# Attention output normalised in 32x32-block transposes on VectorE, in place of two full transposes on TensorE

## The reference

```
x = x + attn_a(layernorm(x))
x = x + ffn(layernorm(x))
x = x + attn_b(layernorm(x))          # causal, rotary
x = x + ffn(layernorm(x))

attn: scores = q k^T / sqrt(16); p = softmax(scores)
      out[b, n, (h d)] = sum_m p[b, h, n, m] v[b, m, h, d];  return out @ out_w^T (+ out_b)
ffn:  gate = sigmoid((x Wq^T) routers^T);  leaf = product of the gates on the path, 256 leaves
      return (leaf @ leaf_values) Wout_w^T + Wout_b
```

## Time and profile before

| | |
|---|---|
| runs | 1141.99, 1144.35, 1144.99 us; median 1144.35 |
| profiled execution | 1141.19 us, span from the first to the last instruction 1139.5 us |
| TensorE clock granted, mean | 0.99 of 2.4 GHz |
| busy: PE, DVE, ACT, POOL | 1075.6, 883.5, 761.6, 307.0 us |
| chain that ended last: PE, DVE, ACT | 59%, 22%, 7% of the span |

### The profile page before, as it was taken

The page is one execution under the profiler, slowest core; times in us unless marked ns, Lnnn a source line. Parts: engine busy times, 40 slices in busy tenths (PEclk is TensorE's granted clock), DMA queues, the critical chain, the costliest instruction groups (busy, mean ns, idle before and its releaser), DMA issues.

```text
span 1139.5 us, 18953 instructions
## 1 busy us (share of the span) xinstructions
PE 1075.6 (94%) x6164; PEld 543.1 (48%) x6164; DVE 883.5 (78%) x2481; ACT 761.6 (67%) x1565; POOL 307.0 (27%) x339
## 2 busy tenths in 40 slices
PE   5899999999999999999999999999999898989986
PEld 3323444444445444554455544454444555545544
DVE  4887787787868897687977878788886878777844
ACT  3577767677776678765777767776776666666562
POOL 3011110114213150222403151131513526262210
PEclk9999999999999999999999999999999999999999
DMA  8150501402205131321305023051311313022001
GB/s 240 49 128 19 130 20 50 99 20 85 83 20 130 38 107 43 99 70 38 111 20 149 20 66 102 19 131 35 103 50 40 110 38 122 28 85 65 20 20 37
DMA packets 79778, 80.97 MB, mean 71 GB/s; under 512 B 13088, under 2 KB 68672, under 8 KB 79680
## 3 DMA queue, kind: packets, MB, share of 16 engines
q1 hardware_dynamic: 79616, 79.73, 24.6%
q0 software_dynamic: 64, 0.03, 0.0%
HBM read 20.71 MB, written 8.39 MB: 26 GB/s over the span
## 4 chain that ended last, share of the span: by engine, by line
PE 59%; DVE 22%; ACT 7%; issue 4%; SPq 3%; POOL 2%; DMA 1%; POOLq 0%; DVEq 0%; ACTq 0%
PE ps_work L1304 13%; PE ps_out L1213 12%; PE ps_max L1167 11%; PE ps_key L1189 11%; DVE neg_max L916 8%; PE ps_work L1343 7%; ACT probs L797 4%; PE ps_work L1269 3%; DVE scratch L1073 3%; DVE ps_max L912 2%; SPq L538 2%; DVE scratch L1103 2%; DVE scratch L1076 2%; ACT turned_block L818 2%; DVE moments L1021 1%
## 5 line engine op out<-in xcount | busy, mean ns | idle before, releaser
L797 ACT ACTIVATE probs<-ps_key 128x512 f32<-128x512 f32 (+3 forms) x1024 | 515.4, 520 | 297.2 <-PE ps_key L1189 291.5
L916 DVE TENSOR_REDUCE neg_max<-ps_max 128x1 bf16<-128x512 f32 x512 | 336.9, 684 | 86.5 <-PE ps_max L1167 85.2
L1167 PE MATMUL ps_max<-k_stack,q_stack 96*128 96x512 bf16 (+3 forms) x1024 | 347.0, 345 | 24.0 <-DVE neg_max L912 10.0
L1189 PE MATMUL ps_key<-q_stack,k_stack 97*128 97x512 bf16 (+3 forms) x1024 | 348.4, 343 | 16.0 <-ACT probs L797 10.5
L912 DVE CUSTOM_DVE_ANT_0 ps_max<-ps_max,mask_b 128x128 f32<-128x128 f32 (+3 forms) x512 | 247.1, 504 | 105.5 <-PE ps_max L1167 102.7
L1213 PE MATMUL ps_out<-probs,v_ones 128*32 128x512 f32 (+3 forms) x2048 | 233.8, 529 | 0.6 <-POOL probs L688 0.6
L1167 PEld LDWEIGHTS ps_max<-k_stack,q_stack 96*128 96x128 bf16 x1024 | 99.4, 97 | 277.1 <-DVE neg_max L916 109.8
L688 POOL TENSOR_SCALAR_AFFINE_SELECT probs<-probs 128x512 f32<-128x512 f32 x128 | 82.2, 643 | 402.3 <-ACT probs L797 401.7
L1189 PEld LDWEIGHTS ps_key<-q_stack,k_stack 97*128 97x128 bf16 x1024 | 100.9, 99 | 139.7 <-ACT probs L797 87.6
L1213 PEld LDWEIGHTS ps_out<-probs,v_ones 128*32 128x32 f32 x2048 | 40.4, 108 | 73.7 <-issue 65.3
L912 DVE DVE_READ_ACCUMULATOR2_ANT neg_max<- 128x1 bf16 x512 | 72.8, 142 | 0.0
(11 more groups left out here) (93 smaller groups left out, 1254.1 us busy)
## 6 DMA issues: line engine op xcount, KB each, us to landing
k_stack<-k_part SPq DMA_DIRECT2D x108, 128.0 KB, 2.4
q_stack<-q_part SPq DMA_DIRECT2D x108, 128.0 KB, 2.4
k_stack<-k_part SPq DMA_DIRECT2D x42, 256.0 KB
q_stack<-q_part SPq DMA_DIRECT2D x42, 256.0 KB
x_in<-in_x SPq DMA_DIRECT2D x8, 512.0 KB, 3.9
q_stack<-shift_rows SPq DMA_DIRECT2D x256, 1.0 KB, 1.7
x_again<-in_x SPq DMA_DIRECT2D x8, 512.0 KB, 3.9
spill<-x_plain SPq DMA_DIRECT2D x8, 512.0 KB, 2.8
```

The source lines that it names most:

```text
L797: act.activation(probs[step % RING][:, j, q0:T], ps_key[slot % 2][:, 0:T - q0], ACT.Exp, scale=SCALE).then_inc(on["exp_done"], 1)
L916: dve.tensor_reduce(out=dst, in_=src, axis=AX_X, op=ALU.max, negate=True)\
L1167: pe.matmul(dst[:, 0:keys], q_stack[n % 2][0:SPLIT_ROWS, h, P * qt:P * qt + P], k_stack[n % 2][0:SPLIT_ROWS, h, 0:keys], start=True, stop= ...
L1189: pe.matmul(ps_key[slot % 2][:, 0:T - q0], k_stack[n % 2][0:STACK_ROWS, h, P * kb:P * kb + P], q_stack[n % 2][0:STACK_ROWS, h, q0:T], star ...
```

## The change

The output is no longer turned to full token rows and back by TensorE. VectorE transposes `out_raw` in 32x32 blocks (`turn_out`, slots 7, 23, 39, 55) to `out_rows`: each block holds 32 tokens down and one head's 16 features and denominator across. One slot later `divide` takes the reciprocals and multiplies into one half of `divided[half]`, where the features of two groups lie side by side. One slot after every second group (slots 9 and 41 in all phases but the first) `turn_back` transposes `divided[half]` in 32x32 blocks to `turned_out`, which the projection reads directly. Since the features now come out in another order, the rows of `a_o` and `b_o` are loaded in that order, by 8 DMAs each at slot 30 of phases 0 and 1; the one product that needs `a_o` in plain order, `bias_fold`, and the first projection read a copy `first_out` loaded at slot 2 of phase 0. The work banks have fewer users. Some steps move by a slot or more in the tables.

```diff
-TURN_LAG = MIX_LAG + 5
+OUT_TURN = 2
...
-    ("bias_input", 0, (), 1), ("bias_input", 1, (), 3), ("turn_attended", 0, (13,), 14),
-    ("turn_attended", 1, (14,), 15), ("project_out", 0, (18, 19), 20), ("moments", 0, (), 21),
-    ("project_out", 1, (21, 22), 23), ("moments", 1, (), 23), ("spread", 0, (), 24), ("turn_block", 0, (30,), 31),
+    ("bias_input", 0, (), 1), ("bias_input", 1, (), 3), ("project_out", 0, (18, 19), 20), ("moments", 0, (), 21),
+    ("project_out", 1, (21, 22), 23), ("moments", 1, (), 23), ("spread", 0, (), 28), ("turn_block", 0, (30,), 31),
...
+def half_of(n, g):
+
+    return (g % 2, g // 2) if n == 0 else (g // 2, g % 2)
...
+                if slot == 30 and n < len(PLACED):
+                    for k in range(KC):
+                        by_place = w[PLACED[n]][P * k:P * k + P, :].rearrange("(e j d) n -> j e d n", e=2, j=GROUP)
+                        for j in range(GROUP):
+                            sp.dma_start(weights[PLACED[n]][COLS * j:COLS * j + COLS, k, :], by_place[j])\
+                              .then_inc(placed_loaded[n], DMA)
...
-            def divide(n, g, bank):
...
-                dve.wait_ge(on["out_turned"], count.next("out_turned"))
-                dve.reciprocal(inverse[:, :, :], turned[:, :, :, DH]).then_inc(on["inverse_done"], 1)
...
+            def turn_out(n, g):
+
+                if count.some("divided"):
+                    dve.wait_ge(on["divided"], count.of("divided"))
+
+                dve.wait_ge(on["out_ready"], count.next("out_ready"))
+                dve.transpose(out_rows[:, :], out_raw[g % 2][:, :]).then_inc(on["out_turned"], 1)
+                count.add("out_turned")
+
+            def divide(n, g):
+                half, odd = half_of(n, g)
...
+                dve.wait_ge(on["out_turned"], count.of("out_turned"))
+                rows = by_block(out_rows)
+                dve.reciprocal(inverse[:, :], rows[:, :, DH]).then_inc(on["inverse_done"], 1)
...
+                dve.tensor_tensor(by_block(divided[half])[:, :, DH * odd:DH * odd + DH], rows[:, :, 0:DH],
+                                  inverse[:, :].unsqueeze(2).broadcast_to([P, T // COLS, DH]), ALU.mult)\
+                   .then_inc(on["divided"], 1)
...
+            def turn_back(n, g):
+                half, odd = half_of(n, g)
+                if odd:
+
+                    dve.wait_ge(on["divided"], count.of("divided"))
+                    dve.transpose(turned_out[:, half, :], divided[half][:, :]).then_inc(on["attended"], 1)
+                    count.add("attended")
...
-            def turn_out(g, begun, bank):
...
-                for qt in range(TILES):
-                    last = pe.transpose(bank[:, P * qt:P * qt + P], out_raw[g % 2][:, P * qt:P * qt + P], ident[:, :])
...
-            def turn_attended(m, i, n, bank, parts):
-
-                pe.wait_ge(on["attended"], count.of("attended"))
-                turn_tiles(attended, i, bank)
...
+                rows(turned_out, weight, i, bank, D, "x_ready", parts, "added_full", "attended")
```

More of the change, by code:

```diff
@@ L390, in by_tile, with by_block @@
             return bank[:, :].rearrange("p (t n) -> p t n", t=2)
[L392 to L393 removed]
+        def by_block(rows):
+            return rows[:, :].rearrange("p (b c) -> p b c", c=COLS)
         on = {name: sem(name) for name in EVENTS}
@@ L949, in core @@
                     largest(n, at)
-                if out_due(n, slot) is not None:
-                    divide(n if slot >= GROUP_SLOTS else n - 1, out_due(n, slot), bank_of["turn_out", n, slot])
+                for lag, step in ((OUT_TURN, turn_out), (OUT_TURN + 1, divide), (OUT_TURN + 2, turn_back)):
+                    due = out_due(n, slot, lag)
+                    if due is not None:
+                        step(*due)
             def opening():
@@ L981, in closing @@
             def closing():
-                divide(PHASES - 1, GROUPS - 1, bank_of["turn_out", PHASES, 0])
+                for step in (turn_out, divide, turn_back):
+                    step(PHASES - 1, GROUPS - 1)
             def add(m, i, bank, src):
@@ L1216, in mixed @@
                 last.then_inc(on["mixed_done"], 1)
-            def turn_out(g, begun, bank):
-                pe.wait_ge(on["out_ready"], count.of("out_ready", begun))
-                take(bank, "attended")
-                for qt in range(TILES):
-                    last = pe.transpose(bank[:, P * qt:P * qt + P], out_raw[g % 2][:, P * qt:P * qt + P], ident[:, :])
-                last.then_inc(on["out_turned"], 1)
             def core(n, slot):
@@ L1228, in core @@
                     ahead(n, at)
-                if out_due(n, slot) is not None:
-                    turn_out(out_due(n, slot), 1, bank_of["turn_out", n, slot])
                 by_key(n, slot)
@@ L1294, in turn_leaves, with rows @@
                 turn_tiles(leaf_probs[(LEVELS - 1) % 2], i, bank)
-            def rows(turned, weight, i, bank, width, read, parts, full):
+            def rows(turned, weight, i, bank, width, read, parts, full, made="turned"):
                 if 0 in parts:
-                    pe.wait_ge(on["turned"], count.of("turned"))
+                    pe.wait_ge(on[made], count.of(made))
                     take(bank, read)
@@ L1311, in project_out @@
             def project_out(m, i, n, bank, parts):
-                rows(turned_block, weights["b_o" if causal(m) else "a_o"], i, bank, D, "x_ready", parts, "added_full")
+                if i == 0 and 0 in parts:
+                    count.add("attended", KC)
+                if m > 0 and i == 0 and 0 in parts:
+                    pe.wait_ge(placed_loaded[1 if causal(m) else 0], DMA * KC * GROUP)
+                weight = first_out if m == 0 else weights["b_o" if causal(m) else "a_o"]
+                rows(turned_out, weight, i, bank, D, "x_ready", parts, "added_full", "attended")
                 added[i] = count.of("x_ready")
```

78 lines of the change are left out of this document (38 added, 40 removed).

## The result

The changed kernel took 1150.2 us (median of 7 runs, 1147.37 to 1152.17) against 1144.03 us for the kernel before (7 runs, 1141.09 to 1146.1). The ratio is 1.0049, 95% interval 1.0032 to 1.0065: 5.6 us slower, where 10 us faster had been forecast. Slower by over 0.3% had a chance of 0.22. The time lies inside the stated range of 1115 to 1155 us, but that range took in both signs, so this says nothing for the forecast.

What follows compares the result with a forecast made beforehand. No single engine was taken to set the pace: TensorE in some stretches, VectorE in others. Gains of 20.5 us less 11 us of added VectorE work gave about 10 us less, 1144.35 to 1134 us; range 1115 to 1155.

Steps and rivals of the forecast that it cites:

- The price of the block transpose: One 128x512 f32 block transpose on VectorE, absent from the trace, was taken at 0.65 us, between bounds 0.60 and 0.83.
- The gain where TensorE paces: TensorE's removed transpose sets on the chain, 0.44 us each: 13.3 - 0.67 + 1.8 us, of 42.2 us in all.
- Slots 7 to 9 of plain phases: VectorE's 1.33 us of new work fits barely into 1.9 us idle; 0.15 us booked in 20 places, 3 us.
- The 0.65 us booked for slots 23 and 39: Added VectorE transposes where VectorE is late (slot 23) or ahead of the next norm's statistics (slot 39): 12 places, 7.8 us.
- Moved table steps and the freed work banks I book at nothing either way: Steps moved in the slot tables and work banks with fewer users: no gain or cost booked.
- the 4.9 us of ScalarE's copies: ScalarE loses 32 copies; ten on the chain at 0.49 us, most after slot 9 of causal phases, gain 4.9 us.
- Slots 55 to 57 in all phases, 23 to 25 in causal ones: VectorE has 2.5 to 6.5 us to spare per group there, so its added transposes cost nothing.
- the end, 1.2 us less: Serial path at the very end: turning, dividing and turning back falls from 3.36 to 2.2 us.
- the clock, named as a sign and booked at nothing: Granted clock below 0.99 as TensorE works less would show the prediction wrong; no time booked.
- VectorE's term: Cost of VectorE's added block transposes on the path: 3 + 7.8 = 10.8, about 11 us.
- Rival 4: Slower, 1161 us: the block transpose is a half-rate pass of 1.22 us; chance 0.22 for the slower side as a whole.

Runs made afterwards that it cites:

- the short block transposes: The changed kernel with both kinds of VectorE block transpose cut to 32 of their 512 columns: ratio 0.988 to the kernel before, 1128.3 us.

## Why the prediction was wrong

**Right.** The price of the block transpose: 0.65 us, measured 0.70 in duration and 0.63 to the next start. The gain where TensorE paces: 0.44 us in three of the four plain groups from slot 53 (0.34 in the last), and 12.8 us over the kernel for 14.4 summed. Slots 7 to 9 of plain phases: the work did fit there, and the groups from slot 5 fell by 0.51 us. The 0.65 us booked for slots 23 and 39 was of the right size: 0.8 us in plain groups from slot 21, and 0.44 in causal ones from slot 37 once `leaves` 1 is back.

**Failed: "Moved table steps and the freed work banks I book at nothing either way".** This step made the kernel slower: `leaves` 1 one slot later costs 5.5 us, and without that the ratio is 1.0001. The forecast's 10 us faster had failed beside it, for the reasons below. Its four short operations had filled a wait of VectorE for TensorE; moved, they leave it idle there and lengthen a row of operations ahead of a maximum. I had read neither which idle time a moved step stood in nor what it is joined with.

**Failed: the 4.9 us of ScalarE's copies.** The count was short to begin with: the chain has 12 such pieces ahead of the closing part, not 10, two in each of phases 1, 2, 4, 6, 8 and 10. In phases 1 and 2 the groups from slot 5 did get 1.0 us shorter each, which is the size of two copies. In causal phases 4 to 10, where eight of them lay (8 x 0.49 = 3.9 us), the groups from slot 5 should have lost about 1 us each, and instead grew by 0.02. ScalarE in the changed kernel, causal phase 6, in order of time:

```profile
473.97 0.63 ACT L903 ACTIVATE q_part<-scratch 128x512 bf16<-128x512 f32 x1 [1.08 <-DVE scratch L1141]
...
476.76 0.63 ACT L903 ACTIVATE q_part<-scratch 128x512 bf16<-128x512 f32 x1 [0.43 <-DVE scratch L1141]
```

In the place of its copies ScalarE now waits for VectorE's remainder of the split (L1141). VectorE and, under it, GpSimd at that place:

```profile
471.52 0.71 DVE L979 STREAM_TRANSPOSE turned_out<-divided 128x512 f32<-128x512 f32 x1
...
472.60 1.34 DVE L1141 TENSOR_TENSOR scratch<-scratch,q_part 128x512 f32<-128x512 f32 x1
```

```profile
470.89 2.50 POOL L782 TENSOR_TENSOR k_part<-scratch,k_part 128x512 bf16<-128x512 f32 x2
473.35 1.08 POOL L706 TENSOR_SCALAR_AFFINE_SELECT probs<-probs 128x512 f32<-128x512 f32 x1
```

The remainder took 0.83 us here before, most of it in a gap of GpSimd's work, and 1.34 now. With the short block transposes it took 0.69 and started 0.74 us earlier, counted from the copy, ScalarE didn't wait for it, and the group came out 0.89 us shorter than before. ScalarE's exponential stands behind that wait and TensorE's next product behind the exponential, in the changed kernel and with the short transposes:

```profile
476.23 0.23 PE L1227 MATMUL ps_key<-q_stack,k_stack 97*128 97x128 bf16 x1 [0.92 <-ACT probs L815]
```

```profile
469.97 0.23 PE L1232 MATMUL ps_key<-q_stack,k_stack 97*128 97x128 bf16 x1 [0.34 <-ACT probs L820]
```

So VectorE's new work took this gain. How much of it by its own length and how much through the slower remainder no run separates.

**Failed: "Slots 55 to 57 in all phases, 23 to 25 in causal ones: TensorE paces ... Cost nothing."** It held for slots 55 to 57 (-0.34 to -0.44 us a group). At slot 23 it didn't: with the moved steps back, the causal groups from slot 21 are 0.23 us longer than before where they should be 0.44 shorter, and moving the transpose off slot 23 gave those 0.67 us back. The 2.5 us to spare that I read were a sum over 16 slots; at slots 20 to 24 there was less to spare than the transpose and the division take.

**Failed: the end, 1.2 us less.** It was 1.5 us more: the path is 0.9 us shorter and the projection, at half clock, 2.6 longer.

**Failed: the clock, named as a sign and booked at nothing.** The prediction said that it is wrong if the granted clock falls below 0.99. It was 0.981 in the profiled execution, for 0.990 before, and 0.978 in the median, which by the line of the kernel before is as much as the whole loss. Where one and the same group of phases 4 to 10 has a stretch at half clock in one trace and none in another with the same places, it is 0.9 to 1.25 us longer (from slot 37) or 1.4 to 1.7 (from slot 5).

**The sum again.** 15.6 us lie between forecast and result. Of these 5.5 are `leaves` 1, 3.9 ScalarE's copies, 2.7 the end and 1.6 the sets of transposes, together 13.7. The other 1.9 would then be VectorE's term, 12.9 for the 11 booked; that is a remainder and wasn't measured, and since phases 1 and 2 gave back up to 2.0 us of copies where 1.0 was booked, it may as well be 2.9. The clock is no further term beside these: 2.6 of the 2.7 us at the end are clock and about 1 of the 5.5, and part of the remainder may be. Rival 4 had the right side by the wrong mechanism, and none of the rivals was a moved step.

**What stays open.** Where the clock falls differs between executions of one kernel, and each kernel has one trace; so how much of each ratio is clock is known only as the line over 90 executions has it, and what of the lower clock is cause and what effect isn't known. The moved steps were tried apart; the new order in which the work banks are taken, booked at nothing in the same sentence, was not.

## What to carry to other kernels

Where a diff changes operations and also moves steps of a schedule, price each move by itself: which idle time the step had filled, and what stands behind it in its new place. Here one step of four short operations cost 5.5 us, where the fastest version gained 11.9. Room on an engine is read in the slots in which new work lands, not as a sum over the stage; with the four steps of causal phases back in their old places, one group's transposes four slots later and TensorE kept busy ahead of the last projection, the same algorithm was 1.04% faster than the kernel before, which had no such retiming of its own. And compare the granted clocks of the executions before reading half a per cent out of two times.

## What the runs showed of the hardware

- Four f32 transposes of 128x128 take 0.44 us of TensorE's time; one f32 block transpose of 128x512 on VectorE lasts 0.70 us, 0.63 to the start of the next operation.
- A VectorE operation with two inputs in SBUF and 512 columns took 0.69 us in a gap of GpSimd's work and 1.34 us beside it.
- Behind 3.14 us in which TensorE idled, the next 16 matmuls took 6.30 us in place of 3.7 (5.25 to 6.40 in ten kernels); 24 idle f32 transposes in that time kept them at 3.7 in four kernels.
- Over 90 executions of one kernel the time rose by 0.67 us for each 0.001 of granted clock less.
